# Output products of a key tile in two halves, with side work and the second scores between them

## The reference

```python
q, k, v = (split_heads(q), split_heads(k), split_heads(v))
score = jnp.einsum('bhqd,bhkd->bhqk', q, k) / jnp.sqrt(jnp.float32(HD))
score = score + (1.0 - mask) * -1000000000.0
alpha = jax.nn.softmax(score, axis=-1)
context = jnp.einsum('bhqk,bhkd->bhqd', alpha, v)
...
x = x + _L0_xattn_ref(_layernorm(x, axis=-1), ctx_1024, ctx_1024, ...)
x = x + _L0_ffn_ref(_layernorm(x, axis=-1), ...)
x = x + _L1_xattn_ref(_layernorm(x, axis=-1), ctx_1024, ctx_1024, ...)
x = x + _L1_ffn_ref(_layernorm(x, axis=-1), ...)
```

## Time and profile before

| | us |
|---|---|
| median of three runs (1304.70 to 1309.87) | 1304.73 |
| the profiled execution | 1301.18 |
| its span, from the first to the last instruction | 1299.4 |
| TensorE busy with matmuls (17942) | 1173.9 (90%) |
| TensorE busy with weight loads (17942) | 583.9 (45%) |
| ScalarE busy | 1037.8 (80%) |
| VectorE busy | 755.3 (58%) |
| GpSimd busy | 175.2 (13%) |

### The profile page before, as it was taken

How to read it: one execution, slowest core, us unless ns; L and a number is a source line. 1 busy time by engine, 2 the same in 40 slices (tenths; PEclk the granted TensorE clock), 3 DMA queues, 4 the chain that set the end, 5 groups by cost and what they waited for, 6 DMA issues and landing times. The chain is left out here.

```text
span 1299.4 us, 43658 instructions
## 1 busy us (share of the span) xinstructions
PE 1173.9 (90%) x17942; PEld 583.9 (45%) x17942; DVE 755.3 (58%) x1655; ACT 1037.8 (80%) x1482; POOL 175.2 (13%) x211
## 2 busy tenths in 40 slices
PE   8888898898898999999899999978989999998994
PEld 5422232232222356677899999742223223222222
DVE  5326767767757676445666666652546445444446
ACT  3599999999999855443566666539999999999992
POOL 5111111011001030333000010132320000000000
PEclk9999999999999999999999999989999999999997
DMA  6236834534546333221343354222120000000001
GB/s 190 66 111 222 264 106 149 166 106 151 176 127 216 94 116 109 87 68 50 106 120 116 114 151 148 60 86 85 46 57 15 22 25 2 21 26 3 2 3 65
DMA packets 106305, 124.94 MB, mean 96 GB/s; under 512 B 25091, under 2 KB 89310, under 8 KB 106142
## 3 DMA queue, kind: packets, MB, share of 16 engines
q1 hardware_dynamic: 89088, 85.95, 21.5%
q0 software_dynamic: 9328, 29.37, 7.2%
q10 hardware_dynamic: 7726, 7.26, 1.9%
HBM read 70.27 MB, written 46.95 MB: 90 GB/s over the span
## 5 line engine op out<-in xcount | busy, mean ns | idle before, releaser
L887 ACT ACTIVATE prob<-banks 128x1024 f32<-128x1024 f32 (+1 forms) x832 | 771.5, 1053 | 8.5 <-PE banks L1675 4.9
L1690 PE MATMUL banks<-prob,v 64*32 64x512 f32 x6656 | 441.8, 592 | 0.6 <-ACT prob L887 0.6
L1675 PE MATMUL banks<-zone,kst 52*32 52x512 f16 x6528 | 336.5, 383 | 86.2 <-ACT prob L887 80.0
L1675 PEld LDWEIGHTS banks<-zone,kst 52*32 52x32 f16 x6528 | 92.7, 89 | 492.9 <-ACT prob L887 476.3
L1690 PEld LDWEIGHTS banks<-prob,v 64*32 64x32 f32 x6656 | 118.6, 106 | 21.3 <-ACT prob L887 2.4
L2309 PE MATMUL banks<-xsT_d,w 128*128 128x128 f16 x1776 | 125.0, 221 | 3.0 <-issue 2.9
L2309 PEld LDWEIGHTS banks<-xsT_d,w 128*128 128x128 f16 x1776 | 110.0, 99 | 11.9 <-issue 8.0
L2320 PE MATMUL banks<-w,hh 128*128 128x256 f16 x592 | 107.0, 273 | 0.0
L1165 DVE RECIPROCAL late<-late 128x512 f32<-128x512 f32 x31 | 103.9, 3353 | 1.1
L2116 DVE TENSOR_TENSOR hl<-hid,hh 128x128 f16<-128x128 f32 x296 | 83.3, 291 | 32.5 <-ACT hh L2047 24.9
L2043 ACT ACTIVATE hid<-banks,b 128x128 f32<-128x128 f32 x222 | 74.7, 369 | 25.6 <-PE banks L2309 21.1
(11 more groups left out here) (280 smaller groups left out, 1295.9 us busy)
## 6 DMA issues: line engine op xcount, KB each, us to landing
weight_parts<-late SPq DMA_DIRECT2D x54, 256.0 KB, 3.5
w<-weight_parts POOLq DMA_DIRECT2D x24, 512.0 KB, 4.0
late<-in_L_ffn_W_r SPq DMA_DIRECT2D x43, 256.0 KB, 3.9
weight_parts<-more SPq DMA_DIRECT2D x26, 256.0 KB, 3.7
zone<-q_parts SPq DMA_DIRECT2D x180, 32.0 KB
slot_rows<-late POOLq DMA_DIRECT2D x14, 384.0 KB, 4.1
more<-in_L_ffn_W_r SPq DMA_DIRECT2D x21, 256.0 KB, 4.3
xs_d<-slot_rows ACTq DMA_DIRECT2D x39, 128.0 KB, 2.1
```

What stands on the lines that cost most here:

```text
L887: nc.scalar.activation(prob[0:m, t % P_RING, 2 * (n % 2):2 * (n % 2) + 2, :], score[G % S_RING][0:m, :, :], ACT.Exp, scale=0.25).then_inc( ...
L1675: last = nc.tensor.matmul(score[G % S_RING][j:j + wide, a, :], kst[stack, 2 * q + n % 2, t * P + j:t * P + j + wide], qst[stack, u % Q_RIN ...
L1690: last = nc.tensor.matmul(outp[u % 2][GROUP * j:GROUP * (j + 1), a, :], v[rows, t, u % NQ, j, :], prob[rows, (u * KT + t) % P_RING, j, :], ...
```

## The change

`outputs` gets a third argument, `part`, and makes the products of 256 of the 512 queries: the same eight matmuls with half the columns. The accumulation is started by the first half of the first tile and ended by the second half of the last. The waits for the accumulators stand ahead of the first half, the wait for the exponentials ahead of both, and `pv_done` is signalled by the second half alone. In the loop the second scores stand between the two halves, and the tile's side stands between the first half and the second scores. The last outputs of a layer are made as two halves in a row.

```diff
-            def outputs(u, t):
-                if t == 0:
+            def outputs(u, t, part):
+                if t == 0 and part == 0:
                     if u >= 2:
                         pe.wait_ge(out_read, u - 1)
                     if sides_before(u):
                         pe.wait_ge(side_free, sides_before(u))
                 pe.wait_ge(exp_done, 2 * (u * KT + t) + 2)
+                cols = slice(part * CH // 2, (part + 1) * CH // 2)
                 for a in range(2):
                     rows = slice(HALF * a, HALF * (a + 1))
                     for j in range(QH):
-                        last = nc.tensor.matmul(outp[u % 2][GROUP * j:GROUP * (j + 1), a, :], v[rows, t, u % NQ, j, :],
-                                                prob[rows, (u * KT + t) % P_RING, j, :], start=(t == 0), stop=(t == KT - 1),
+                        last = nc.tensor.matmul(outp[u % 2][GROUP * j:GROUP * (j + 1), a, cols], v[rows, t, u % NQ, j, :],
+                                                prob[rows, (u * KT + t) % P_RING, j, cols], start=(t == 0 and part == 0), stop=(t == KT - 1 and part == 1),
                                                 tile_position=(HALF * a, GROUP * j))
-                last.then_inc(pv_done, 1)
+                if part:
+                    last.then_inc(pv_done, 1)
...
                     if G < UNITS * PAIRS:
                         scores(G)
                     if u or t:
-                        outputs((u * KT + t - 1) // KT, (t - 1) % KT)
+                        outputs((u * KT + t - 1) // KT, (t - 1) % KT, 0)
+                    if t and t in pieces:
+                        side(*pieces[t])
                     if G + 1 < UNITS * PAIRS:
                         scores(G + 1)
-                    if t in pieces:
+                    if u or t:
+                        outputs((u * KT + t - 1) // KT, (t - 1) % KT, 1)
+                    if t == 0 and t in pieces:
                         side(*pieces[t])
-            outputs(UNITS - 1, KT - 1)
+            for part in range(2):
+                outputs(UNITS - 1, KT - 1, part)
```

## The result

| | before | after |
|---|---|---|
| median, us | 1307.14 (1304.70 to 1309.87, 4 runs) | 1327.72 (1324.45 to 1332.26, 4 runs) |
| ratio, 95% interval | | 1.0156 (1.0134 to 1.0178) |
| profiled execution, us | 1301.18 | 1324.45 |
| its span, us | 1299.4 | 1322.7 |

The change makes the kernel slower by 20.6 us at the medians. The forecast was 1319, 14.3 above the 1304.73 it was set against, with a range up to 1332: the direction and the range held, the size was a third too small. In the changed kernel the outputs are L1691, "out" is L1718, a turn L1725, half a wave L1752.

What follows compares the result with a forecast made beforehand. ScalarE's exponentials were taken to bound both attention layers. The side's shared gap 13.6, a wait 0.5 and layer starts -0.45 sum to 13.7, say +14 us: 1315 from the profiled 1301.2, stated as 1319 against the 1304.7 median; range 1309 to 1332.

Steps and rivals of the forecast that it cites:

- What bounds the kernel: Both attention layers: ScalarE's exponentials set the pace, 0.904 us apart; 25.6 of 1299.4 us are lost to late starts.
- Step (1): Outputs on TensorE: a half takes 0.43 us, two stream as long as the whole, and doubled weight loads stay covered.
- rival C: Outputs' weight loads uncovered: 0.11 us more in each half, 13 us on top, 1332 us; chance 0.07.
- Step (2): Second scores behind the first half, tiles without a side: ready 0.66 us after the first, then wait; gives nothing.
- Step (3): Side before second scores, 0.55 us after the half starts, all in one gap: loss 35.7 against 22.1, +13.6 us.
- Rival A: Side needs no drain behind a half, starting 0.33 us after it, not 0.55: faster, 1292 us; chance 0.06.
- B: Second of two neighbouring sides still shares the first one's delay: +8 us, about no change, 1310; chance 0.14.
- Step (4): Waits of sides: no new ones, but the query waiting for VectorE at 136.38 now holds back scores: +0.5 us.
- Step (5): First outputs at 1.2 GHz, half moved behind second scores: -0.45 us a layer, between 0 and -0.85; first layer's swallowed.
- Rival D: TensorE's instruction supply limits tiles of 48 load-and-matmul pairs at 62 ns each: 490 us more; chance 0.03.
- gaps without a releaser on TensorE: Sign on TensorE's timeline that would show the forecast wrong and instruction supply, priced at 490 us, to be the limit.

Runs made afterwards that it cites:

- without the traffic: First layer's expert-weight loads (from the fourth piece) and routed stores (but the first expert's) cut to an eighth; with the kernel before otherwise unchanged, 1305.84 us.
- after_less_traffic: The changed kernel with most of the first layer's expert-weight loads and stores cut to 16 of 128 partitions; 1321.3 us, ratio 1.0117.
- scores in halves: The kernel before, whole outputs and its order, but scores made in two halves of 256 queries, one behind the other; 1321.22 us, ratio 1.0110.
- halves_old_order: Outputs in two halves in a row, in the order of the kernel before (scores, half, half, scores, side); 1316.04 us, ratio 1.0078.
- sides_spread: Kernel before with outputs split only in side-free tiles behind a side, plus sides moved to every second tile in both layers; 1309.06 us, ratio 1.0014.

## Why the prediction was right, and where it was too low

- *What bounds the kernel*: right. ScalarE's pace is unchanged (0.90 between undelayed exponentials), and all of the loss shows as scores that come late.
- *Step (1), the halves*: the streaming was right, 0.86 for two halves in a row and 0.46 for one (1005.49 to 1005.95), and rival C (a half over 0.5) is out. The price of nothing was not: halves alone cost 9.0 us, some 2.6 of it, in the profiled execution, the longer wait for VectorE. What was costed was the time to run a half, not the time to deliver its instructions.
- *Step (2)*: right, the second scores of a tile without a side are 0.91 behind the first.
- *Step (3), the side in one gap*: right in mechanism and size. Half to side measured 0.55, and the order cost 15.5 us without the traffic, against 13.6. From the sixth unit of the second layer on, where the DMA share is 0.04, it is 278.15 - 269.92 = 8.2 us. Rival A (a side 0.43 or less after a half) is out, and so is B: the second of two neighbouring waves costs what the first does (in after_less_traffic, at 1069 and 1071 us, 1.271 and 1.266 us between exponentials, 0.36 above the pace where 0.38 was forecast).
- *Step (4), the query that waits for VectorE*: right, it waits 1.07 us at 134.70 and the exponential behind it is 2.42 after the one before, where it was 2.01: 0.4 for the 0.5 forecast.
- *Step (5), layer starts*: the sixth exponential of the first layer starts 54.61 - 49.72 = 4.89 after the first, where it was 5.74: -0.85, the far bound, where -0.45 was taken; the second layer's does the same. The first unit keeps it (23.99 us against 24.86; without the traffic 24.92 against 25.41). Whether the wait for VectorE swallows it, as forecast, can't be read, because a late packet lies between. The error is 0.4 us a layer.
- *Rival D*: here the sum went wrong. The prediction asked whether TensorE can issue 48 pairs in a tile, found a scores group whose eight loads run in 0.11 us, and gave instruction supply 0.03. It did not ask where the instructions come from. The trace of before had it: queue q8 with 125 packets, and stretches of the first layer with a DMA busy share of over 0.9 (134 to 138 us). The term is not 490 us but 4 to 5 for the changed kernel, and 9 less 2.4 = 6.6 for halves alone, less the 2.6 of the wait for VectorE. The sign "gaps without a releaser on TensorE" was the right one, and it showed.
- *The range*: that 1327.7 fell inside it is partly luck. Its upper end, 1332, stood for a round of 0.25 and for uncovered weight loads, and neither came; what came was a term given next to nothing. Without it the sum would have been close: 13.7 against 15.5.

The Trainium skill, "Runtime: NRT & Kernel Launch", section "Instruction fetch mechanics", says that an engine's instructions arrive in blocks of 16 KiB, 256 instructions, which the packets here bear out, and that fetching them is hidden behind their dispatch. The runs differ on the second: it was hidden with 125 packets (no group of matmuls in the layers stops for a microsecond in either profile of before), and with 177 it cost some 4 to 5 us, in the layer that shares the DMA engines with the weights.

What stays open: how much of the first layer's 8.2 us in scores in halves is late packets, since no kernel without the traffic was run for it; and what makes scores late beside GpSimd's gathers in some executions and not in others. A kernel without the gathers was not tried.

## What to carry to other kernels

Splitting an operation doubles its instructions even where it costs the engine nothing; look up the instruction queue's packets and the DMA's busy share in that stretch before you price it at zero. A gap of one pace holds one piece of extra work: what decides is not how much TensorE has to do but what stands between two scores, so put the split where a delay has already happened, not where the side is. And take the "before" of a comparison from more than one profile, stretch by stretch: 6 us of the second layer's difference here belonged to one execution.

## What the runs showed of the hardware

- TensorE's instructions take 64 bytes each (52 packets of 16384 bytes for 13312), and it goes on 1.2 to 1.6 us after a late packet has landed (eleven pauses in six runs). What it holds ahead is little: from the start of the packet of 406.89 to the stop it ran 516 instructions, before four other pauses (in after and halves_old_order) 335 to 476, which makes, as an estimate, no more than about two packets of 256.
- Waits that are already over follow each other on TensorE 0.106 us apart when they are instructions of their own (eleven between outputs and scores); one record lasts 51 ns. The 17 ns of ScalarE are such a record's duration and not a spacing, so they were the wrong figure to price TensorE's by.
- The fourth unit's wait for VectorE is a chain: VectorE waits for a piece of weights (1.73 and 3.28 us), reads the accumulators behind that, and TensorE's query waits for it. After waits of 1.93 us (halves_old_order) and 3.68 us (sides_spread) TensorE's granted clock was 0.50, its 1.2 GHz level, in the stretch behind.
